# Layer 0 of a fused two-layer transformer kernel: projection moved ahead of two transposes on TensorE, exponentials moved up on ScalarE

## The chip, the cores and the metric

The kernel runs on one core of a Trainium2 chip. The metric is the device time of one execution in microseconds; the time of the kernel before is the median of three executions.

## The reference, cut to what matters

The input is x, 16 sequences of 512 rows of 128 numbers, float32. Two layers follow, each an attention block and a mixture-of-experts block with a residual sum and a layer norm behind each. The change touches only layer 0, whose attention runs between the 16 heads of one row (a 16x16 softmax per row, not between rows), so that rows are independent:

```python
qkv = einsum('bnm,fm->bnf', x, Wqkv)             # per row: 16 heads x (q, k, v) of 8
scores = einsum('bnhd,bngd->bnhg', q, k) / 8.0    # 16 x 16 for every row
attn = softmax(scores, axis=-1)
out = einsum('bnhg,bngd->bnhd', attn, v)
x1 = layernorm(x + out @ Wproj.T + bproj)
logits = x1 @ gate_w.T + gate_b                   # keep the top 2 of 8, softmax
x2 = layernorm(x1 + sum_e gate[e] * (x1 @ expert_w[e] + expert_b[e]))
```

Layer 1 (causal-masked attention with 16 heads, then a routed expert block) is not changed.

## The kernel before, in words

`layer0` (L66) works on pairs of 128-row tiles: 64 tiles, so NP = 32 pairs. It is software-pipelined over five stages: step s starts the attention scores of pair s, sums the heads and projects pair s-1, does the gates and expert products of pair s-2, sums the experts and does the second norm of pair s-3, and makes layer 1's value rows of pair s-4. Each engine has its own hand-written order of these pieces (a function `step` per engine); the flags `part[n]` say which stages exist in the first and last steps. Engines are tied by counting semaphores only, and each engine issues in its written order, so a piece that waits holds everything written behind it on the same engine. In the text, "the pair's" wait counts are left out.

The pieces that matter here, by engine:

- VectorE (DVE). `moments_1` (L639, L643) takes mean and variance of the projected rows in `ps_front` and waits for the projection's semaphore `r1_ps`. Then `exp_sums` (L735) and `exp_recips` (L742), which wait for ScalarE's exponentials; `qk_products` (L661, two of 2.2 us), `moments_2` (L651, L655), `gate` (L676 to L704), `qk_sums` (L713, 4.43 us), `find_max` (L719) and `shift_scores` (L726), which ends the step and sets `scores_shifted`.
- GpSimd (POOL). `inverse1` (L288 to L296) waits for `moments_1` and makes rstd and shift of the first norm; `normalise` (L266) makes the probabilities; `pv_products` (L274, two of 4.1 us) multiplies them with the values; `inverse2` (L302 to L310) and `bias_residual` (L316) follow.
- TensorE (PE). `sum_experts` (L422 to L429, of pair s-3) opens the step; it waits for `gT_sb` (the turned gates copied to SBUF) and for `scores_shifted`. Then `values` (L451), `turn_x1` (L388), `turn_r2` (L437), `logits` (L403, L405), `four_experts` (L396) for the first tile, `qkv_products` (L352), `sum_heads` of the first tile (L364, 16 transposes that accumulate), `qkv_products`, `four_experts(1, 0)`, `sum_heads` of the second tile, `four_experts(1, 1)`, and at the end of the step `turn_gates` (L414), `turn_x2` (L444) and `project` (L377, L379), which sets `r1_ps`. `turn_gates` and `project` both wait for `oT_sb`, the copy of the summed heads.
- ScalarE (ACT). The end of its step is `apply_gates(1, 0)` (L541), `norm2` (L562), `copy_oT` (L504, sets `oT_sb`), `copy_gT` (L549, sets `gT_sb`), `apply_gates(1, 1)` (L541), `copy_x2T` (L570) and `exponentials` (L511, two of 256 columns; each waits for its half of `scores_shifted`). The next step opens with `norm1` (L519), `copy_r2T` (L555) and `copy_x1T` (L526).
- SyncE loads `xT` and the residual rows two steps ahead and stores the turned second norm; its waits are on `qkv_ps`, `r1_ps` and `x2T_sb`.

The PSUM areas at stake: `ps_front` holds the projection (columns 0 to 255) and the logits, `ps_turn` the summed heads and, in its other half, in turn the turned x1 and the turned gates, `ps_scores` the scores and then the summed experts of another pair. So `sum_experts` can only write after the scores have been read by `shift_scores`.

Of the kernel before, what the change touches and what calls it, by code (L numbers as in the profile page):

```python
# [34 lines left out]
def when(eng, semaphore, count):  # L35

    if not isinstance(count, int) or count > 0:
        eng.wait_ge(semaphore, count)  # L38
# [27 lines left out]
def layer0(nc, sh, xT_in, wqkv, wproj, bproj, gate_w, gate_b, expert_w, expert_b, wv1, wqT, wkT, bq, keep):  # L66
# [7 lines left out]
    with ExitStack() as ctx:  # L74
# [116 lines left out]
        def before(u, j, k):  # L191

            return u + (j - k) // 2, (j - k) % 2

        def first(u, j, s):

            return isinstance(u, int) and 2 * u + j == s
# [3 lines left out]
        def tile(t, a, n=P):  # L201
            return t[:, a * n:(a + 1) * n]

        with nc.Block() as block:
# [129 lines left out]
            def _(pe):  # L334
                pe.wait_ge(wqkv_in, 16)

                def build_matrices():
                    pe.wait_ge(qk_weights_in, 16 * 3)
                    for g in range(H // 4):
                        for h in range(4 * g, 4 * g + 4):  # L340
                            mm = pe.matmul(tile(ps_m[g], h % 4), tile(wq, h), tile(wk, h), start=True, stop=True)
                        mm.then_inc(m_ps, 1)
                    pe.wait_ge(m_sb, 1)
                    for h in range(H):
                        mm = pe.matmul(ps_m[0][:, h:h + 1], tile(wk, h), bq_sb[:, h:h + 1], start=True, stop=True)
                    mm.then_inc(mb_ps, 1)
# [21 lines left out]
                def project(u, j):  # L368
                    s = 2 * u + j
                    pe.wait_ge(oT_sb, s + 1)  # L370
                    pe.wait_ge(xres_biased, s + 1)
                    if first(u, j, 0):
                        pe.wait_ge(m_sb, H // 4)
                    when(pe, x1_ready, 2 * s)
                    when(pe, gates_ready, s)
                    for a in range(2):
                        pe.matmul(tile(ps_r1, a), tile(attnT, a), wproj_sb[:, :], start=(a == 0), stop=False)  # L377
                    for a in range(2):
                        mm = pe.matmul(tile(ps_r1, a), tile(xres[j], a), ident[:, :], start=False, stop=(a == 1),  # L379
                                       is_transpose=True)  # L380
                    mm.then_inc(r1_ps, 1)
# [9 lines left out]
                def four_experts(u, j, a, half):  # L391
                    s = 2 * u + j
                    if first(u, j, 0):
                        pe.wait_ge(mb_sb, 1)
                    when(pe, gated_ready, 4 * s + 2 * a + half - 1)
                    pe.matmul(ps_y[half][:, :], tile(x1T, a), expw_sb[:, half * 4 * P:(half + 1) * 4 * P],  # L396
                              start=True, stop=True).then_inc(experts_ps, 1)
# [10 lines left out]
                def turn_gates(u, j):  # L408

                    s = 2 * u + j  # L410
                    pe.wait_ge(gates_ready, s + 1)
                    pe.wait_ge(oT_sb, min(s + 2, NP) if isinstance(s, int) else s + 2)
                    for a in range(2):
                        mm = pe.transpose(tile(ps_gT, a), tile(gates, a, E), ident[:, :])  # L414
                    mm.then_inc(gT_ps, 1)

                def sum_experts(u, j):

                    s = 2 * u + j
                    pe.wait_ge(gT_sb, s + 1)  # L420
                    pe.wait_ge(scores_shifted, 2 * min(s + 3, NP) if isinstance(s, int) else 2 * (s + 3))
                    pe.matmul(ps_r2T, expb_sb[:, :], gatesT[:, :], start=True, stop=False)  # L422
                    for a in range(2):
                        pe.matmul(tile(ps_r2T, a), tile(x1[j], a), ident[:, :], start=False, stop=False,
                                  is_transpose=True)
                        for e in range(E):
                            if e % 4 == 0:
                                pe.wait_ge(gated_ready, 4 * s + 2 * a + e // 4 + 1)
                            mm = pe.matmul(tile(ps_r2T, a), tile(gated[a], e), ident[:, :], start=False,  # L429
                                           stop=(a == 1 and e == E - 1), is_transpose=True)  # L430
                        mm.then_inc(r2T_ps, 1)
# [22 lines left out]
                def step(u, j, part):  # L454
                    if first(u, j, 1):
                        build_matrices()
                    if part[4]:
                        sum_experts(*before(u, j, 3))
                    if part[5]:
                        values(*before(u, j, 4))  # L460
                    if part[3]:
                        turn_x1(*before(u, j, 2))
                    if part[4]:
                        turn_r2(*before(u, j, 3))
                    if part[3]:
                        logits(*before(u, j, 2))
                        four_experts(*before(u, j, 2), 0, 0)
                        four_experts(*before(u, j, 2), 0, 1)
                    if part[0]:
                        qkv_products(*before(u, j, -1), 0)  # L470
                    if part[2]:
                        sum_heads(*before(u, j, 1), 0)
                    if part[0]:
                        qkv_products(*before(u, j, -1), 1)
                    if part[3]:
                        four_experts(*before(u, j, 2), 1, 0)
                    if part[2]:
                        sum_heads(*before(u, j, 1), 1)
                    if part[3]:
                        four_experts(*before(u, j, 2), 1, 1)  # L480
                        turn_gates(*before(u, j, 2))
                    if part[4]:
                        turn_x2(*before(u, j, 3))
                    if part[2]:
                        project(*before(u, j, 1))
                qkv_products(0, 0, 0)
                qkv_products(0, 0, 1)
                pe.wait_ge(consts_made, 5)
# [4 lines left out]
            def _(act):  # L493
# [6 lines left out]
                def copy_oT(u, j):  # L500
                    s = 2 * u + j
                    act.wait_ge(pv_summed, 2 * (s + 1))
                    when(act, r1_ps, s)
                    act.copy(attnT[:, :], ps_oT).then_inc(oT_sb, 1)  # L504

                def exponentials(u, j):
                    s = 2 * u + j
                    when(act, probs_ready, s)
                    for a in range(2):
                        act.wait_ge(scores_shifted, 2 * s + a + 1)  # L510
                        act.activation(tile(exps, a, HH), tile(shifted, a, HH), ACT.Exp, scale=0.125)\  # L511
                           .then_inc(exps_ready, 1)
# [76 lines left out]
                def step(u, j, part):  # L589
                    if first(u, j, 1):  # L590
                        copy_matrices()
                    if part[3]:
                        norm1(*before(u, j, 2))
                    if part[4]:
                        copy_r2T(*before(u, j, 3))
                    if part[3]:
                        copy_x1T(*before(u, j, 2))
                    if part[5]:
                        copy_v(*before(u, j, 4))
                    if part[3]:  # L600
                        gate_exp(*before(u, j, 2))
                    if part[0]:
                        copy_kv(*before(u, j, -1), 0)
                    if part[3]:
                        apply_gates(*before(u, j, 2), 0, 0)
                        apply_gates(*before(u, j, 2), 0, 1)
                    if part[0]:
                        copy_kv(*before(u, j, -1), 1)
                    if part[3]:
                        apply_gates(*before(u, j, 2), 1, 0)  # L610
                    if part[4]:
                        norm2(*before(u, j, 3))
                    if part[2]:
                        copy_oT(*before(u, j, 1))
                    if part[3]:
                        copy_gT(*before(u, j, 2))
                        apply_gates(*before(u, j, 2), 1, 1)
                    if part[4]:
                        copy_x2T(*before(u, j, 3))
                    if part[1]:  # L620
                        exponentials(u, j)
                copy_kv(0, 0, 0)
                copy_kv(0, 0, 1)
                steps(act, step)
# [1402 lines left out]
```

## Time and profile before

| what | value |
|---|---|
| median of 3 runs | 2204.5 us (2201.29 to 2204.99) |
| profiled execution | 2212.01 us, span 2210.3 us |
| busy in the span: PE, DVE, ACT, POOL | 93%, 81%, 71%, 48% |
| layer 0 in the span | about the first 550 us, 32 steps |

The profiled execution is one execution under the profiler, 1.7 us longer than its own span and 7.5 us above the median. In the rows below a time is counted from the start of the span, "us" is the busy time of a merged group, "x" the number of instructions in it, and the bracket at the end is the idle time of that engine just before the group and what ended it. PEld is TensorE's weight load, which can overlap its matmuls. Matmuls overlap one another by a part of their modelled length, so a group's cost is read from the start of one group to the start of the next.

### The profile page before, as it was taken

How to read it: one execution, taken by the hardware profiler on the slowest of the kernel's cores; microseconds unless marked ns; L12 is line 12 of the kernel's file. 1: busy time of each engine (PE TensorE's matmuls, PEld its weight loads, DVE VectorE, ACT ScalarE, POOL GpSimd, SP SyncE). 2: the span in 40 equal slices, each digit the busy share in tenths (PEclk: the TensorE clock that was granted, in tenths of full speed). 3: DMA queues.
4: the chain of work that ended last, by engine and by line, in shares of the span. 5: the costliest groups of instructions: out<-in, count | busy, mean ns of one | idle time of the engine just before them, and what ended most of it. 6: DMA issues, size and time to landing. Idle time of an engine off the chain costs nothing. (4 is left out here: it accounts for less than half of the span.)

```text
span 2210.3 us, 59748 instructions
## 1 busy us (share of the span) xinstructions
PE 2054.5 (93%) x16112; PEld 1527.0 (69%) x16112; DVE 1785.9 (81%) x5918; ACT 1559.9 (71%) x3951; POOL 1060.8 (48%) x2184
## 2 busy tenths in 40 slices
PE   7999999997999999999999999999999993999990
PEld 5666666665676766776676676676677663999990
DVE  7899999994788888888888888888888884677765
ACT  3565656565788877878787887787887872777764
POOL 5777777775223334344334334333434434444444
PEclk8999999999999999999999999999999996999995
DMA  2000000000000000000000000000200001222217
GB/s 76 23 23 27 21 28 21 28 21 15 13 2 9 4 11 11 2 12 11 3 10 11 7 6 11 9 4 11 88 2 11 11 3 39 66 65 63 67 57 228
DMA packets 63632, 62.84 MB, mean 28 GB/s; under 512 B 9834, under 2 KB 58613, under 8 KB 62855
## 3 DMA queue, kind: packets, MB, share of 16 engines
q1 hardware_dynamic: 54906, 42.64, 6.4%
q0 software_dynamic: 8448, 16.93, 2.2%
q8 instruction: 121, 1.98, 0.4%
q14 instruction: 157, 1.29, 0.2%
HBM read 33.17 MB, written 22.69 MB: 25 GB/s over the span
## 5 line engine op out<-in xcount | busy, mean ns | idle before, releaser
L1367 DVE SCALAR_TENSOR_TENSOR restT<-ps_t,leadT 128x512 f16<-128x512 f32 (+1 forms) x768 | 458.8, 597 | 135.1 <-ACT leadT L1294 97.7
L1294 ACT ACTIVATE leadT<-ps_t 128x512 f16<-128x512 f32 (+1 forms) x768 | 402.8, 525 | 131.8 <-PE ps_t L1168 131.7
L1151 PE MATMUL ps_s<-xT_all,qm 128*128 128x512 f32 (+1 forms) x1024 | 490.0, 560 | 0.8 <-ACT qm L1275 0.8
L1168 PEld LDWEIGHTS ps_t<-ident,p 128*128 128x128 f32 x2560 | 314.8, 141 | 238.7 <-issue 171.5
L1168 PE MATMUL ps_t<-ident,p 128*128 128x128 f32 x2560 | 415.2, 276 | 9.3 <-DVE restT L1367 5.8
L1285 ACT ACTIVATE p<-ps_s,neg_max 128x512 f32<-128x512 f32 (+1 forms) x512 | 326.1, 637 | 88.3 <-DVE neg_max L1357 74.2
L987 POOL CAST v_parts<-v_all 128x36 bf16<-128x36 f32 x256 | 57.4, 224 | 614.5 <-PE ps_o L1182 614.3
L1357 DVE CUSTOM_DVE_ANT_0 ps_s<-ps_s,mask 128x512 f32<-128x512 f32 (+1 forms) x512 | 319.8, 625 | 38.5 <-PE ps_s L1151 37.4
L1151 PEld LDWEIGHTS ps_low<-xT_all,qm 128*128 128x128 f32 x1024 | 194.6, 190 | 135.4 <-issue 122.2
L1142 PE MATMUL ps_qm<-xT_all,m_all 128*128 128x512 f32 x512 | 263.7, 597 | 3.2 <-PEq L765 3.2
L274 POOL TENSOR_TENSOR pv_prod<-probs,kv 128x2048 f32<-128x2048 f32 x64 | 259.5, 4076 | 3.8 <-POOL probs L266 2.3
L1668 POOL DMA_INDIRECT results<-row_out,row_in x136 | 133.7, 983 | 161.8 <-issue 121.0
L1151 PE MATMUL ps_low<-xT_all,qm 128*128 128x256 f32 (+1 forms) x1024 | 208.9, 326 | 0.0
L1275 ACT ACTIVATE qm<-ps_qm,mb_all 128x512 f32<-128x512 f32 x256 | 176.1, 688 | 43.2 <-PE ps_qm L1142 39.8
L1285 ACT ACTIVATE p<-ps_low,neg_max 128x256 f32<-128x256 f32 (+1 forms) x512 | 188.3, 428 | 0.1
L1357 DVE CUSTOM_DVE_ANT_0 ps_low<-ps_low,mask 128x256 f32<-128x256 f32 (+1 forms) x512 | 177.8, 387 | 9.7 <-PE ps_low L1151 1.4
L541 ACT ACTIVATE gated<-ps_y,gates 128x128 f32<-128x128 f32 x512 | 141.7, 371 | 44.1 <-DVE gates L704 41.6
L1789 DVE SCALAR_TENSOR_TENSOR e_hid<-e_ps_u,e_wide,e_silu 114x128 f32<-114x128 f32 x408 | 118.4, 345 | 60.3 <-ACT e_silu L1748 55.4
L1182 PE MATMUL ps_o<-v_parts,leadT 128*128 128x27 bf16 x2560 | 161.4, 175 | 0.9 <-DVE restT L1367 0.6
L1182 PE MATMUL ps_o<-v_parts,restT 128*128 128x27 bf16 x2560 | 160.6, 174 | 0.0
L1073 POOL DMA_INDIRECT rows_dram<-rows,slot_idx x128 | 128.9, 1007 | 63.8 <-issue 50.2
L1748 ACT ACTIVATE e_silu<-e_ps_g,e_wide 114x128 f32<-114x128 f32 x408 | 120.3, 366 | 54.4 <-PE e_ps_g L1701 51.0
(231 smaller groups left out, 4161.2 us busy)
## 6 DMA issues: line engine op xcount, KB each, us to landing
row_in<-rows_dram SPq DMA_DIRECT2D x136, 65.0 KB
y<-results SPq DMA_DIRECT2D x16, 512.0 KB, 5.3
xT<-in_xT SPq DMA_DIRECT2D x32, 128.0 KB, 2.1
xres<-in_xT SPq DMA_DIRECT2D x32, 128.0 KB, 2.1
xT_all<-x2T SPq DMA_DIRECT2D x32, 128.0 KB, 2.0
out_x<-x SPq DMA_DIRECT2D x16, 256.0 KB, 3.5
xT_all<-in_wide SPq DMA_DIRECT2D x1, 2760.0 KB
results<-row_out,row_in POOLq DMA_INDIRECT x136
```

What stands on the lines that cost most here:

```text
L274: pool.tensor_tensor(tile(pv_prod, a, HH * DH).rearrange("p (g h d) -> p g h d", g=H, d=DH), tile(probs, a, HH).rearrange("p (h g) -> p g ...
L541: last = act.activation(tile(gated[a], e), tile(ps_y[half], e % 4), ACT.Copy, scale=gates[:, a * E + e:a * E + e + 1])
L1142: pe.matmul(ps_qm[:, :], blk(m_all, h), xT_all[:, bass.ds(b * S, S)], start=True, stop=True).then_inc(qm_ps, 1)
L1151: mm = pe.matmul(ps_s[n], qm[j][:, n * P:(n + 1) * P], xT_all[:, bass.ds(b * S, (n + 1) * P)], start=True, stop=True)
L1168: mm = pe.transpose(ps_t[g][:, at + n * P:at + (n + 1) * P], probs[i][:, n * P:(n + 1) * P], ident[:, :])
L1182: mm = pe.matmul(out_ps[:, i, :], part[:, at + n * P:at + (n + 1) * P], v_parts[j][:, n * PARTS * PV:(n + 1) * PARTS * PV], start=(n == 0 ...
L1275: act.activation(qm[j][:, :], ps_qm[:, :], ACT.Identity, bias=mb_all[:, h:h + 1], scale=SCALE).then_inc(qm_sb, 1)
L1285: act.activation(probs[i][:, :], ps_s[i], ACT.Exp, bias=neg_max[:, i:i + 1], scale=-1.0).then_inc(probs_ready[i], 1)
L1294: act.activation(leadT[j][g][:, :], ps_t[g][:, 0:width[g]], ACT.Copy, scale=RAISE)\
L1357: dve.tensor_tensor_reduce(out=ps_s[i], in0=ps_s[i], in1=mask[:, S - n:S], scale=-1.0, scalar=3e38, op0=ALU.add, op1=ALU.min, accum_out=ne ...
L1367: dve.scalar_tensor_tensor(out=restT[j][g][:, :], in0=ps_t[g][:, 0:width[g]], scalar=RAISE, in1=leadT[j][g][:, :], op0=ALU.mult, op1=ALU.s ...
L1668: pool.indirect_dma_start(out=results[:, :], out_offset=bass.IndirectOffsetOnAxis(ap=row_in[r][:, P + 1:ROW].bitcast(U32), axis=0), in_=ro ...
```

## The change

On TensorE `project` of pair s-1 moves from the end of the step to just behind `four_experts(1, 1)`, ahead of `turn_gates` and `turn_x2`. On ScalarE `exponentials` of pair s moves from the end of the step to just behind `copy_oT`, ahead of `copy_gT`, `apply_gates(1, 1)` and `copy_x2T`. No instruction is added or removed, and every wait stays with its instruction.

```diff
@@ -478,11 +478,12 @@
                         sum_heads(*before(u, j, 1), 1)
                     if part[3]:
                         four_experts(*before(u, j, 2), 1, 1)
+                    if part[2]:
+                        project(*before(u, j, 1))
+                    if part[3]:
                         turn_gates(*before(u, j, 2))
                     if part[4]:
                         turn_x2(*before(u, j, 3))
-                    if part[2]:
-                        project(*before(u, j, 1))
                 qkv_products(0, 0, 0)
@@ -612,13 +613,13 @@
                         norm2(*before(u, j, 3))
                     if part[2]:
                         copy_oT(*before(u, j, 1))
+                    if part[1]:
+                        exponentials(u, j)
                     if part[3]:
                         copy_gT(*before(u, j, 2))
                         apply_gates(*before(u, j, 2), 1, 1)
                     if part[4]:
                         copy_x2T(*before(u, j, 3))
-                    if part[1]:
-                        exponentials(u, j)
                 copy_kv(0, 0, 0)
```

## Rows read from the trace of the kernel before

**Rows 1.** Busy time in one window, 26 steps of layer 0; PEclk is the granted clock.

```profile
core 0: us, PE busy (x) PEld busy (x) DVE busy (x) ACT busy (x) POOL busy (x), PEclk, DMA share, GB/s
99.64:511.98 412.34, 382.63 (x2285) 268.53 (x2284) 376.60 (x780) 242.66 (x857) 315.32 (x312) 1.00 0.08 25
```

**Rows 2.** Waits, 99 to 497 us: who waited for whom, total us, times, longest.

```profile
POOL var L288 <- DVE mv L643: 86.5, 25, 3.6
...
DVE stats L639 <- PE ps_front L379: 11.9, 26, 0.5
...
DVE exp_sum L735 <- ACT exps L511: 2.4, 13, 0.2
```

**Rows 3.** Waits of VectorE, 40 to 99 us, in the first steps.

```profile
DVE stats L639 <- PE ps_front L379: 5.2, 3, 3.0
```

**Rows 4.** Timeline of VectorE: start us, busy us, group, [idle before, releaser].

```profile
98.88 0.76 DVE L726 TENSOR_TENSOR shifted<-ps_scores,score_max 128x256 f32<-128x256 f32 x2
...
306.34 0.50 DVE L639 BATCH_NORM_STATS2 stats<-ps_front 128x6 f32<-128x128 f32 x2 [0.43 <-PE ps_front L379]
...
321.00 0.76 DVE L726 TENSOR_TENSOR shifted<-ps_scores,score_max 128x256 f32<-128x256 f32 x2
322.26 0.49 DVE L639 BATCH_NORM_STATS2 stats<-ps_front 128x6 f32<-128x128 f32 x2 [0.51 <-PE ps_front L379]
...
511.23 0.75 DVE L726 TENSOR_TENSOR shifted<-ps_scores,score_max 128x256 f32<-128x256 f32 x2
```

**Rows 5.** Timeline of GpSimd, one step and the start of the next.

```profile
307.45 0.20 POOL L288 TENSOR_TENSOR var<-mv,eps_pair 128x2 f32<-128x2 f32 x1 [3.59 <-DVE mv L643]
...
309.96 8.12 POOL L274 TENSOR_TENSOR pv_prod<-probs,kv 128x2048 f32<-128x2048 f32 x2 [0.18 <-POOL probs L266]
...
323.27 0.20 POOL L288 TENSOR_TENSOR var<-mv,eps_pair 128x2 f32<-128x2 f32 x1 [3.33 <-DVE mv L643]
...
325.66 8.11 POOL L274 TENSOR_TENSOR pv_prod<-probs,kv 128x2048 f32<-128x2048 f32 x2
```

**Rows 6.** Timeline of TensorE's matmuls, the same step and the next.

```profile
318.14 1.97 PE L364 MATMUL ps_turn<-ident,pv_prod 128*128 128x128 f32 x16
319.94 1.02 PE L396 MATMUL ps_y<-expw_sb,x1T 128*128 128x512 f32 x2
320.80 0.38 PE L414 MATMUL ps_turn<-ident,gates 128*8 128x128 f32 x2
...
321.24 0.61 PE L377 MATMUL ps_front<-wproj_sb,attnT 128*128 128x128 f32 x4
...
322.00 0.69 PE L422 MATMUL ps_scores<-gatesT,expb_sb 8*128 8x256 f32 x2
...
324.64 0.61 PE L451 MATMUL ps_turn<-wv_sb,x2T 128*128 128x128 f32 x4
325.55 0.44 PE L388 MATMUL ps_turn<-ident,x 128*128 128x128 f32 x2 [0.29 <-ACT x L519]
...
327.31 1.96 PE L396 MATMUL ps_y<-expw_sb,x1T 128*128 128x512 f32 x4
329.11 0.81 PE L352 MATMUL ps_qkv<-wqkv_sb,xT 128*128 128x384 f32 x2
```

**Rows 7.** Timeline of TensorE's weight loads in the step after, one row.

```profile
336.34 0.08 PEld L414 LDWEIGHTS ps_turn<-ident,gates 128*8 128x8 f32 x1 [0.43 <-ACT attnT L504]
```

**Rows 8.** Weight loads of line 377, 99 to 497 us: ns min/median/max.

```profile
L377 PEld LDWEIGHTS ps_front<-wproj_sb,attnT x104: 186/192/192, 98.9 to 496.0; 128*128 128x128 f32 x104
```

**Rows 9.** Timeline of ScalarE around the end of the same step.

```profile
321.22 0.36 ACT L549 COPY gatesT<-ps_turn 8x256 f32<-8x256 f32 x1 [0.65 <-PE ps_turn L414]
321.49 1.10 ACT L541 ACTIVATE gated<-ps_y,gates 128x128 f32<-128x128 f32 x4
...
322.76 0.72 ACT L511 ACTIVATE exps<-shifted 128x256 f32<-128x256 f32 x2
324.69 0.81 ACT L519 ACTIVATE x<-ps_front,shift,rstd 128x128 f32<-128x128 f32 x2 [1.21 <-POOL shift L296]
```

## The prediction

> **What bounds the kernel now.** I read four views, in this order. First the busy windows: over 26 steps of layer 0 TensorE is busy 383 of 412 us and VectorE 377, at a granted clock of 1.00, the 2.4 GHz level [rows 1]. Neither share says which of them sets the step. Second, the waits: VectorE waits for the projection in each of 26 steps, 11.9 us in all, and 13 times for the exponentials, 2.4 us; GpSimd waits 86.5 us for VectorE's moments [rows 2]. Third, the timelines of the engines over one step, to find a closed loop: a chain of waits that comes back to the same instruction one step later. Fourth, the ends of steps: from the 98.88 to the 511.23 row of L726 lie 26 steps, 15.86 us each [rows 4].
>
> The loop closes through GpSimd, TensorE and VectorE. GpSimd's `inverse1` starts at 307.45, its head products end at 309.96 + 8.12 = 318.08: 10.63 us [rows 5]. TensorE's `sum_heads` follows at 318.14 (0.06), `four_experts(1,1)` at 319.94 (1.80), `turn_gates` at 320.80 (0.86), `project` at 321.24, past `turn_gates` and `turn_x2` (0.44) [rows 6]. VectorE's statistics start at 322.26 (1.02) [rows 4], and GpSimd's next `inverse1` at 323.27 (1.01) [rows 5]. The sum is 15.82, the distance of the two `inverse1` rows, with no slack in any link. The steps alternate a little, so I use the mean of 15.86. VectorE has slack: after `shift_scores` ends, which I call E (321.00 + 0.76 = 321.76, and 306.34 - 0.43 = 305.91 a step earlier), it is idle 0.51 and 0.43 us [rows 4].
>
> **The change, part by part.**
>
> 1. *`project` ahead of `turn_gates` and `turn_x2`.* In the loop the link of 0.44 us goes: 15.86 becomes 15.42. Its waits move with it. `oT_sb` was waited for by `turn_gates` as well, so nothing new stands ahead of it; in the step after the one shown that copy ended last before the first weight load [rows 7]. The projection's first weight load now stands directly behind that copy: 0.19 us [rows 8] in place of 0.08 [rows 7]. If all is exposed, 0.11 us in every second step, 0.05 per step; if hidden, 0. I take 0.05, since the load did start only after the copy: **15.47 us per step**. The Trainium skill ("TensorE: Matmul & The Clock Gate", the table at its head) says that TensorE pulls weight loads ahead of matmuls in flight; by that rule the load would cost nothing and the step would be 15.42. In the row of the trace the load didn't pass its own wait, so I hold to the row.
>
> 2. *`turn_gates`, `turn_x2` behind it.* They start some 0.8 us later in the stream (the projection's own length, 322.00 - 321.24 [rows 6]), but nobody but ScalarE waits for them: `copy_gT` and `copy_x2T`. The next point covers both.
>
> 3. *`exponentials` ahead of `copy_gT`, `apply_gates(1,1)` and `copy_x2T`.* Gain: the sum of exponentials on VectorE no longer waits, 2.4 us in 13 waits [rows 2], but VectorE is not the loop that binds, so in the sum this is 0; it lowers VectorE's own bound. Cost: ScalarE now stands from the end of `copy_oT` until the shifted scores come at E, and `copy_gT` behind it. The second exponential starts about E + 0.1 (as `norm1` at 324.69 stood 0.1 behind its releaser), both take 0.72, so the second 0.36, then `copy_gT` 0.36, and 0.08 until TensorE [rows 9]: `sum_experts` starts at **S = E + 0.9**, where it was E + 0.24 (322.00) [rows 6]. It waited for the shifted scores before too, so 0.66 us is lost there, and TensorE stands behind it. `apply_gates(1,1)` takes 1.10 [rows 9] and then ends about S + 1.1; `sum_experts` needs it only for its last four of 18 transposes, over 2 us after S, so it doesn't bind. SyncE's store of x2 comes later with `copy_x2T` and the residual load earlier with `r1_ps`; the first has a whole step before its buffer is used again, the second is waited for a step later. Both cost 0; should that cover fail, a load takes 2 us and would be seen as a wait of POOL L316 or ACT L570.
>
> 4. *Who is behind S.* TensorE from S on: `sum_experts` 2.64 (322.00 to 324.64), `values` until 325.25, then `turn_x1`, which waited 0.29 for `norm1` and started at 325.55; 1.76 to `four_experts` at 327.31; 1.80 to `qkv_products` at 329.11, 0.81 at most; `sum_heads` 1.80; `qkv_products` 0.81; `four_experts(1,0)` 0.86; and then the second `sum_heads` [rows 6]. Without waits that is 3.25 + 1.76 + 1.80 + 0.81 + 1.80 + 0.81 + 0.86 = 11.08 us, so `sum_heads` can start at S + 11.1 = E + 12.0. Today it starts at E + 12.23 (318.14 - 305.91). The closed loop that this makes takes two steps: 12.0 to `sum_heads`, 1.80 and 0.86, 1.02 to the statistics, and from there VectorE's own work to the next E, 321.76 - 306.34 = 15.42 (0.16 of it is the wait for exponentials in every second step, so 15.34): 31.02 / 2 = 15.51. Taken with 0.65 for each `qkv_products` (three quarters of the 0.86 of a 512-column product, 384 columns [rows 6]), it is 15.35. So this loop is as long as the first within a tenth, and `norm1` is no part of it, since it waits for GpSimd's shift [rows 9].
>
> 5. *VectorE alone.* Its own work is 15.34 plus 0.03 between instructions: 15.37 us. No step can be shorter.
>
> **Sum.** The step is the longest of 15.47, 15.35 to 15.51, and 15.37: I take 15.47, from 15.86, 0.39 us over 26 steps, 10.1 us. The first steps wait for the projection too, three times [rows 3]; each gives 0.44: 1.3 us. In the last two steps VectorE has nothing to hide behind; there the earlier projection may give up to 0.44 and the later `sum_experts` take as much, I take 0. Together 11.4 us. Against the profiled execution's own 2212.0 that is 2200.6; the median of the runs shown is 7.5 lower, 2204.5, so **2193 us**. Everything behind layer 0 only starts earlier.
>
> **Rivals.**
>
> - *Partly given back.* `sum_experts` starts later than E + 0.9, say E + 1.2 by slower hand-overs between ScalarE and TensorE, and the two-step loop gives 15.65: 0.21 times 26 and 1.3, some 7 us, 2197.5. For it: the tie within a tenth. Against it: my sum for that loop already takes busy lengths. Chance 0.15.
> - *No change.* The moved wait takes the gain: S at E + 1.5 gives 15.8 us per step, 2202. It shows as `turn_x1` waiting for nothing, and VectorE's wait for the projection as long as now. Chance 0.11. The part of the change on TensorE would then have been worth 0.44, and the part on ScalarE cost it.
> - *VectorE as the bound.* If the longer weight load is hidden and GpSimd's products follow at once, the step is 15.37: 0.49 times 26 and 1.3, 14 us, 2190.5. I count it with the forecast.
> - *Slower.* The place is ScalarE between `copy_oT` and `copy_gT`. Written order makes `copy_gT` stand behind a wait for VectorE's last instruction of the step; the two-step loop passes today's 31.76 as soon as S is over E + 1.65. Should `sum_experts` in effect also need `apply_gates(1,1)` and `copy_x2T` (1.10 and 0.35 later, E + 2.35), the loop is 32.5, the step 16.2, 0.36 longer, and with 26 steps 9 us are added: 2214. Against it: the row of `copy_gT` is 0.36 long and nothing else stands ahead of it. Chance 0.06. The Trainium skill ("TensorE: Matmul & The Clock Gate", the table at its head) says that ScalarE's queue is strictly first in, first out; that is what makes this rival possible, and the rows of the kernel before can't show it, as `copy_gT` there stands behind nothing that waits.
>
> **How the numbers follow.** The forecast, a step of 15.37 to 15.55 us, has 0.68. With 0.15 for the part given back, faster by more than 0.2% (4.4 us, about what a measurement of this kernel tells from no change) has 0.83, within 0.2% has 0.11, slower 0.06. The predicted time is the likeliest case's. The range goes from VectorE's bound of 15.37 with the last steps' gain and the runs' own spread of 2 us, 2188, to just short of no change, 2202; about 2 in 10 is left out above and a little below.
>
> **What would show it.** Right: in the new profile VectorE's wait at L639 falls from 0.46 us a step to about 0.1, its wait at L735 is gone, L377 starts directly behind L396, and steps are 15.4 to 15.5 us apart. ScalarE waits at L511 for L726 instead of at L549, TensorE waits about 0.5 us at L422 for ScalarE's `gatesT`, and less than before at L388 for x1. Right too if GpSimd's wait at L288 gets shorter by about the step's gain. The forecast is wrong if TensorE's second `sum_heads` starts later than 0.1 to 0.2 us behind GpSimd's products in most steps: then the loop over `sum_experts` has taken over. It is wrong in another way if the steps get shorter and the total doesn't, or if the granted clock leaves 1.00 in layer 0, now that TensorE has a new gap ahead of `sum_experts`.

## The result, and the profile after

The changed kernel takes 2186.64 us (median of 4 runs, 2185.8 to 2188.25) where the kernel before took 2204.74 (median of 4 in the same session): a ratio of 0.9923, 95% interval 0.9911 to 0.9934. Faster, as forecast, but by 18.1 us where 11.4 had been worked out, and 1.4 us below the range.

The profiled execution took 2186.65 us (span 2184.9), so it stands for its median. That of the kernel before, 2212.0, stood 7.3 us above its own, and the two spans must not be compared whole.

Busy times of the changed kernel in the window of [rows 1]; the last column but two is the granted clock:

```profile
99.64:511.98 412.34, 385.71 (x2354) 278.39 (x2354) 375.26 (x800) 254.52 (x880) 323.98 (x322) 1.00 0.08 24
```

The shares hardly move; more instructions fit into the same window (2354 matmuls for 2285), which now reaches 18.8 us past the last `shift_scores`. Waits of the changed kernel, 99 to 497 us, answering to [rows 2]:

```profile
POOL var L288 <- DVE mv L644: 77.2, 26, 3.1
...
ACT exps L512 <- DVE shifted L727: 23.3, 26, 0.9
...
PEld ps_turn L364 <- POOL pv_prod L274: 21.2, 27, 1.0
...
PE ps_scores L422 <- ACT gatesT L550: 13.1, 26, 0.5
...
DVE stats L640 <- issue: 2.1, 12, 0.2
...
DVE stats L640 <- PE ps_front L379: 0.3, 1, 0.3
```

VectorE's wait for the projection falls from 11.9 us to 0.3 us under its name and 2.1 us that the profile calls "issue", 0.1 us a step together (the probe below shows that these too are the projection); its wait for the exponentials is gone, ScalarE now waits for VectorE at the exponentials (0.9 us a step), and TensorE waits 0.5 us a step for `gatesT` at the start of `sum_experts`. All four were forecast.

VectorE's timeline of the changed kernel, answering to [rows 4]:

```profile
93.70 0.75 DVE L727 TENSOR_TENSOR shifted<-ps_scores,score_max 128x256 f32<-128x256 f32 x2
...
309.02 0.76 DVE L727 TENSOR_TENSOR shifted<-ps_scores,score_max 128x256 f32<-128x256 f32 x2
309.84 0.50 DVE L640 BATCH_NORM_STATS2 stats<-ps_front 128x6 f32<-128x128 f32 x2
...
324.23 0.75 DVE L727 TENSOR_TENSOR shifted<-ps_scores,score_max 128x256 f32<-128x256 f32 x2
325.15 0.49 DVE L640 BATCH_NORM_STATS2 stats<-ps_front 128x6 f32<-128x128 f32 x2 [0.17 <-issue]
...
493.21 0.75 DVE L727 TENSOR_TENSOR shifted<-ps_scores,score_max 128x256 f32<-128x256 f32 x2
```

From 93.70 to 493.21 lie the same 26 steps as in [rows 4]: 399.5 us where it was 412.35, so 12.8 us came from there, 0.49 per step (15.37 for 15.86). The sixth step itself ends 5.2 us earlier (93.70 for 98.88). Together the last `shift_scores` is 18.0 us earlier. So all of the 18 us is in layer 0, and 5.2 us of it in its first steps, where I had put 1.3.

The loop in the changed kernel, first on GpSimd, then TensorE's matmuls, then the weight loads of `project`:

```profile
310.85 0.20 POOL L288 TENSOR_TENSOR var<-mv,eps_pair 128x2 f32<-128x2 f32 x1 [2.89 <-DVE mv L644]
...
313.24 8.11 POOL L274 TENSOR_TENSOR pv_prod<-probs,kv 128x2048 f32<-128x2048 f32 x2
```

```profile
320.33 1.13 PE L396 MATMUL ps_y<-expw_sb,x1T 128*128 128x512 f32 x2
321.40 1.97 PE L364 MATMUL ps_turn<-ident,pv_prod 128*128 128x128 f32 x16
323.21 1.02 PE L396 MATMUL ps_y<-expw_sb,x1T 128*128 128x512 f32 x2
324.07 0.61 PE L377 MATMUL ps_front<-wproj_sb,attnT 128*128 128x128 f32 x4
324.51 0.38 PE L379 MATMUL ps_front<-ident,xres 128*128 128x128 f32 x2
324.73 0.38 PE L414 MATMUL ps_turn<-ident,gates 128*8 128x128 f32 x2
324.95 0.38 PE L444 MATMUL ps_tail<-ident,x 128*128 128x128 f32 x2
325.86 0.47 PE L422 MATMUL ps_scores<-gatesT,expb_sb 8*128 8x256 f32 x1 [0.53 <-ACT gatesT L550]
```

```profile
323.88 0.60 PEld L377 LDWEIGHTS ps_front<-wproj_sb,attnT 128*128 128x128 f32 x4 [0.48 <-ACT attnT L505]
```

`inverse1` at 310.85, the products end at 321.35 (10.50), `sum_heads` 0.05 behind, `four_experts` 1.81, `project` 0.86, the statistics (325.15) 1.08. The projection follows the expert product directly, and no link has slack: this is still the loop that sets the step. `sum_experts` starts at E + 0.88 (325.86 against 324.98), where the forecast had E + 0.9.

### The profile page after: what moved, and what is told of

Same layout as the page of the kernel before. It is cut to its first block and busy times, and to the rows that moved or that the text cites. A ratio compares the mean times of both kernels' runs of the same rounds, so it can differ in the third digit from the quotient of the medians.

```text
span 2184.9 us, 59761 instructions
## 1 busy us (share of the span) xinstructions
PE 2037.5 (93%) x16112; PEld 1524.8 (70%) x16112; DVE 1778.6 (81%) x5918; ACT 1563.4 (72%) x3951; POOL 1060.6 (49%) x2184
## 5 line engine op out<-in xcount | busy, mean ns | idle before, releaser
L1358 DVE CUSTOM_DVE_ANT_0 ps_low<-ps_low,mask 128x256 f32<-128x256 f32 (+1 forms) x512 | 177.2, 386 | 12.6 <-PE ps_low L1152 1.8
```

What stands on the lines that cost most here:

```text
L1358: dve.tensor_tensor_reduce(out=ps_s[i], in0=ps_s[i], in1=mask[:, S - n:S], scale=-1.0, scalar=3e38, op0=ALU.add, op1=ALU.min, accum_out=ne ...
```

## The experiments

Two questions: do the parts add up and which loop binds now, and where do the first steps' 5.2 us come from? The kernels before and after were also run again as they are, under other names; the ratios are against the kernel before on the same chip.

**TensorE's move alone.**

```diff
                         four_experts(*before(u, j, 2), 1, 1)
+                    if part[2]:
+                        project(*before(u, j, 1))
+                    if part[3]:
                         turn_gates(*before(u, j, 2))
                     if part[4]:
                         turn_x2(*before(u, j, 3))
-                    if part[2]:
-                        project(*before(u, j, 1))
```

> Theory A (the two moves need each other): the gates are turned 0.8 us later, so copy_gT, apply_gates(1,1), copy_x2T and behind them the exponentials end some 6.3 us behind GpSimd's head products; with 0.9 us to the reciprocals and 9.35 us to the next products a new loop of 16.6 us per step takes over from 15.86: about 20 us slower than before, 2225, and VectorE waits over 1 us per step at the sum of exponentials. Rival B (the moves are independent, TensorE's is worth 0.44 per step alone): 2192.

Measured 2220.68 us, ratio 1.0076 (1.0062 to 1.0090): slower by 17 us, where about 20 was expected. ScalarE's timeline of this kernel and then its waits, 99 to 490 us:

```profile
308.89 0.37 ACT L505 COPY attnT<-ps_turn 128x256 f32<-128x256 f32 x1
310.64 0.36 ACT L550 COPY gatesT<-ps_turn 8x256 f32<-8x256 f32 x1 [1.37 <-PE ps_turn L414]
...
311.92 0.35 ACT L571 COPY x2T<-ps_tail 128x256 f32<-128x256 f32 x1
312.17 0.72 ACT L512 ACTIVATE exps<-shifted 128x256 f32<-128x256 f32 x2
```

```profile
ACT gatesT L550 <- PE ps_turn L414: 31.5, 23, 1.4
DVE exp_sum L736 <- ACT exps L512: 28.9, 24, 1.3
POOL probs L266 <- DVE exp_rec L743: 22.8, 24, 1.0
```

The gates are turned later, ScalarE stands 1.37 us for them with the exponentials behind it, VectorE waits for these and GpSimd for VectorE. The steps are 16.47 us apart, where 16.6 was expected. The early projection by itself is a loss.

**ScalarE's move alone.**

```diff
                         copy_oT(*before(u, j, 1))
+                    if part[1]:
+                        exponentials(u, j)
                     if part[3]:
                         copy_gT(*before(u, j, 2))
                         apply_gates(*before(u, j, 2), 1, 1)
                     if part[4]:
                         copy_x2T(*before(u, j, 3))
-                    if part[1]:
-                        exponentials(u, j)
```

> Theory A: the loop over GpSimd, TensorE and the statistics is untouched, 15.86 us per step, so no change within 2 us of before (2203 to 2207), though VectorE's wait at the sum of exponentials is gone and its wait at the statistics grows by as much. Rival B (the later sum of experts costs time by itself): slower by 0.1 to 0.3 us per step, 2208 to 2213.

Measured 2200.2 us, ratio 0.9989 (0.9980 to 0.9998), 3.5 us below the kernel before and about 3 us below the range expected. The steps give little of it: they are 15.82 us apart, 0.04 less, about 1 us in all. The rest fits a better start of 6 of the 11 runs (2199.42 to 2200.2; see the first steps below), though no trace shows the start of those six. VectorE's wait at the statistics took over what it had waited for the exponentials, as expected (99 to 490 us of this kernel; the kernel before has 11.6 there):

```profile
DVE stats L639 <- PE ps_front L379: 13.4, 25, 0.6
```

In the steps by itself a trifle, together with the other move it turns a loss of 0.6 us per step into a gain of 0.49. The two parts aren't two terms of a sum; the second is what makes the first pay.

**One pair of transposes back in the loop.**

```diff
                         four_experts(*before(u, j, 2), 1, 1)
+                        turn_gates(*before(u, j, 2))
                     if part[2]:
                         project(*before(u, j, 1))
-                    if part[3]:
-                        turn_gates(*before(u, j, 2))
```

> Both moves, but turn_gates stays ahead of project: 0.22 us more on TensorE in the loop over GpSimd and the statistics. Theory (that loop and VectorE's own work are both at 15.38 in the changed kernel, tied): the step is 15.38 plus 0.15 to 0.22, so 4 to 6 us over the changed kernel, 2190.5 to 2192.5, and VectorE waits at the statistics again, 0.15 to 0.25 per step. Rival (VectorE alone sets the step, the loop has slack of 0.2 or more): 2186.

Measured 2197.7 us, ratio 0.9972 (0.9963 to 0.9982). The steps are 15.64 us apart, 0.26 more than in the changed kernel for 0.22 us of work, and VectorE waits 0.37 us a step for the projection. Per step that is a bit over the theory's upper end, and the rival's slack of 0.2 us is not there: the loop has no slack at all. The median is 5 us above the 2190.5 to 2192.5 expected. Against a trace of the changed kernel that began alike (`after_third`, below) layer 1 starts 7.6 us later, 545.46 for 537.84; the rest of the 11 us between the medians fits how often the runs had the better start.

**A third of a microsecond more on VectorE.** One more reciprocal behind `exp_recips`, its result not used.

```diff
                     dve.reciprocal(exp_rec[:, :], exp_sum[:, :]).then_inc(recips_ready, 1)
+                    dve.reciprocal(probe[:, :], exp_sum[:, :])
```

> The changed kernel with one more reciprocal of 128x32 on VectorE behind exp_recips (its result is not used), 0.27 to 0.35 us per step, outside the loop over GpSimd. Theory (VectorE's own work sets the step as much as that loop): 0.27 to 0.35 times 30 more, 8 to 10.5 us, 2194.5 to 2197. Rival (only the loop over GpSimd and TensorE sets it): within 1.5 us of 2186.3.

Measured 2187.69 us, 1.4 over the changed kernel's 2186.3: the rival's answer, and my theory of a tie fell. VectorE's timeline of this kernel, and then TensorE's matmuls:

```profile
311.55 0.75 DVE L728 TENSOR_TENSOR shifted<-ps_scores,score_max 128x256 f32<-128x256 f32 x2
312.23 0.50 DVE L641 BATCH_NORM_STATS2 stats<-ps_front 128x6 f32<-128x128 f32 x2
...
314.04 0.30 DVE L745 RECIPROCAL probe<-exp_sum 128x32 f32<-128x32 f32 x1
314.25 4.42 DVE L663 TENSOR_TENSOR qk_prod<-ps_qkv,kv 128x2048 f32<-128x2048 f32 x2
```

```profile
322.93 1.13 PE L397 MATMUL ps_y<-expw_sb,x1T 128*128 128x512 f32 x2
323.89 1.91 PE L365 MATMUL ps_turn<-ident,pv_prod 128*128 128x128 f32 x16
325.64 1.02 PE L397 MATMUL ps_y<-expw_sb,x1T 128*128 128x512 f32 x2
326.50 0.61 PE L378 MATMUL ps_front<-wproj_sb,attnT 128*128 128x128 f32 x4
```

The probe takes 0.21 us of issue (314.04 to 314.25), and the steps are 15.44 us apart, 0.06 more. Here the statistics start 0.07 us *before* the shifted scores end (312.23 against 311.55 + 0.75), or level with that end in every second step; in the changed kernel they start 0.06 or 0.17 behind it. Those gaps, which the profile calls no wait or "issue", were the wait for the projection: in the changed kernel the statistics start 1.02 or 1.08 us behind `project`, the same as in the kernel before, where the profile names it. VectorE's own work is thus at most 15.44 - 0.21 = 15.23 us a step, not 15.37, and the changed kernel stands at least 0.15 us above it.

This doesn't show that VectorE alone sets the step of the probed kernel, because there too the statistics start 1.02 or 1.08 us behind `project`. What sets it is a third loop, which neither the prediction nor the theory above had: from the statistics over the probe to the end of VectorE's `gate` 9.31 us, to ScalarE's `apply_gates(0, 0)` 0.19, to TensorE's `four_experts(1, 0)` 1.20, `sum_heads` 0.96, `four_experts(1, 1)` 1.75, `project` 0.86, and to the statistics (327.58) 1.08. That is 15.35 us for this step and by the same links 15.54 for the next, 15.44 in the mean. The second `sum_heads` starts 0.15 us behind GpSimd's products (323.89 against 323.74) instead of 0.05. In the changed kernel `sum_heads` stood 1.07 behind `four_experts(1, 0)` (320.33 to 321.40), so there this loop had slack: it takes 15.23 where the step is 15.38, and of the probe's 0.21 us only 0.06 came through.

**`copy_gT` ahead of the exponentials**, both moves kept.

```diff
                         copy_oT(*before(u, j, 1))
+                    if part[3]:
+                        copy_gT(*before(u, j, 2))
                     if part[1]:
                         exponentials(u, j)
                     if part[3]:
-                        copy_gT(*before(u, j, 2))
                         apply_gates(*before(u, j, 2), 1, 1)
```

> Both moves, but copy_gT stays ahead of the exponentials on ScalarE: the sum of experts starts some 0.3 us earlier and the exponentials end about 0.7 us later. Theory (TensorE's later sum of experts has slack, and VectorE needs the exponentials only 0.9 us behind its last shifted scores): same as the changed kernel within 1.5 us, 2185 to 2188. Rival (the later sum of experts is what sets the step): 0.1 to 0.3 us per step faster, 2178 to 2183. Second rival (the exponentials have no slack): slower, 2190 or more.

The steps are 15.38 us apart, as in the changed kernel, though `sum_experts` starts 0.25 us earlier (E + 0.6). So the loop over `sum_experts` doesn't bind. The median is 2190.5, outside the 2185 to 2188 expected; its best run is 2185.23. The difference lies in the first steps: its trace is level with the trace of the changed kernel that began alike (`after_third`), layer 1 starting at 537.39 against 537.84.

**The first steps.** The two kernels again, unchanged:

> The kernel before, unchanged, for a second trace. If the earlier start of the third step in the trace of the changed kernel (3.2 us at the end of step 2) came from TensorE's clock in the first 60 us and not from the change, this trace has another split: granted clock in 20 to 60 us differs by trace, and the start of the first projection (33.31 us in the first trace, 30.11 in the changed kernel's) moves with it. If it came from the change, it is 33.3 again. Steps behind 100 us are 15.86 us apart either way.

> The changed kernel, unchanged, for a second trace: steps 15.38 us apart behind 100 us; the first projection starts at 30.1 us if the first steps gained by the change, at 30 to 33.5 if by the clock. Ratio to before 0.992 as in the first runs.

> The changed kernel once more, for how often its runs start with TensorE at the higher level. If the start is chance and alike in both kernels, most of these runs lie near 2188 to 2190, as most runs of the kernel before lie near 2204 (7 of 53 at 2200.5 or below). If the changed kernel starts well more often for a reason of its own, most lie at 2185.5 to 2186.7, as 7 of its 9 did.

Windows of the kernel before in its first trace, in its second, and of the changed kernel in `after_again` and `after_third`; the third number from the end is the granted clock, 1.00 the level of 2.4 GHz:

```profile
20.00:30.00 10.00, 10.00 (x59) 9.29 (x58) 7.80 (x5) 1.73 (x4) 7.48 (x3) 0.66 0.01 2
...
50.00:60.00 10.00, 9.00 (x45) 5.88 (x45) 8.14 (x24) 3.91 (x13) 7.25 (x7) 0.87 0.05 16
```

```profile
20.00:30.00 10.00, 9.54 (x79) 8.67 (x78) 7.79 (x5) 2.66 (x7) 7.48 (x3) 1.00 0.01 2
30.00:40.00 10.00, 6.17 (x18) 3.71 (x19) 8.60 (x23) 2.10 (x7) 7.89 (x7) 0.66 0.08 26
...
50.00:60.00 10.00, 9.02 (x39) 5.43 (x38) 9.55 (x20) 4.68 (x16) 9.92 (x7) 0.83 0.01 2
```

```profile
20.00:30.00 10.00, 9.54 (x78) 8.67 (x77) 7.86 (x5) 2.85 (x8) 7.55 (x3) 1.00 0.01 2
30.00:40.00 10.00, 6.17 (x19) 3.62 (x18) 8.79 (x23) 1.91 (x6) 8.08 (x7) 0.66 0.09 26
...
50.00:60.00 10.00, 9.57 (x51) 5.84 (x50) 9.55 (x20) 5.32 (x20) 9.84 (x7) 1.00 0.01 2
```

```profile
20.00:30.00 10.00, 10.00 (x59) 9.29 (x59) 7.84 (x5) 1.73 (x4) 7.52 (x3) 0.67 0.01 2
```

Each kernel has two starts. In one the clock falls to the lower level within 20 to 30 us, while TensorE runs the one-column products of L345; in the other it falls only in the next ten, where TensorE waits for the first norms. Nothing that the change moves has run by then. A trace between the two exists: in `vector_probe` the clock fell at about 25 us, behind those products. With the start alike:

| trace | clock, 20 to 30 us | sixth `shift_scores` | last | first product of layer 1 |
|---|---|---|---|---|
| before, first | 0.66 | 98.88 | 511.23 | 551.99 |
| after_third | 0.67 | 97.69 | 497.11 | 537.84 |
| before_again | 1.00 | 95.17 | 507.27 | 547.99 |
| after_again | 1.00 | 93.13 | 492.59 | 533.34 |

The change is worth 14.15 us with the one start and 14.65 with the other: 12.6 to 12.9 in the 26 steps, 1.2 to 2.0 ahead of them. The starts of a pair are alike to 0.3 us only (the first projection begins at 33.31 and 33.59, and at 29.87 and 29.68; in `after_third` the clock was at the lower level before 20 us too); with that taken off, the change is worth 14.4 and 14.5. The start itself is worth 4.0 and 4.5 us. The gain ahead of the 26 steps lies mostly in the fifth step, 1.3 us shorter in both pairs. The clock may have a part in what came ahead of the 26 steps: between 52 and 62 us it falls to the lower level for some 3 us in all three traces of the kernel before (the third is `before_filled`, below) and in none of the changed kernel, 0.83 against 1.00 between 50 and 60 us in the windows above. No run separates this from the shorter wait.

The medians were 2203.46 and 2186.27 for the second runs and 2186.94 for the third, 16.5 to 17.2 us apart. The kernel before has 8 of the 62 runs beside these experiments at 2200.5 us or below and most near 2204; the changed kernel has 10 of 14 at 2185.5 to 2187 and 4 at 2188 to 2191. Read as starts, by analogy with the traced runs, this says that the changed kernel had the better one more often, and that is the other 2 to 4 us. Compared within a cluster, the distance is the 14 us of the table: the fastest run of the kernel before is 2199.62, that of the changed kernel 2185.55. Whether the change brings the better start about, the runs don't tell: going by their times the kernel before had it in 3 of the 11 runs of `before_again`, `exps_only` in 6 of 11, `copy_gT` ahead of the exponentials in 1 of 6 and `project` behind the gates in 1 of 9.

**The start made alike.** Sixteen products between the one-column ones, in both kernels, their results not used.

```diff
                     for h in range(H):
+                        pe.matmul(tile(ps_m[0], 1), tile(wk, h), tile(wk, h), start=True, stop=True)
                         mm = pe.matmul(ps_m[0][:, h:h + 1], tile(wk, h), bq_sb[:, h:h + 1], start=True, stop=True)
```

> The kernel before with 16 more products of 128 columns between the one-column products of L345 in step 1 (their results are not used), some 3.5 us more of TensorE there. If the clusters of the kernel before (2199.6 to 2200.4 and 2203.5 to 2206) come from the clock falling behind those one-column products, the granted clock stays at 1.00 from 20 to 30 us, the runs form one cluster, and the median is 2200 plus 0 to 3.5. If not, the two clusters remain, and everything is up to 3.5 later.

> The changed kernel with the same filling. If the change is worth 14.7 us where the clock of the first 60 us is alike (12.6 in the steps behind 100 us and 2.0 ahead of them), this is 14.7 below the filled kernel before, within 1; if the change is worth the 17.4 of the medians by itself, it is 17.4 below.

Measured 2204.48 us (11 runs, 2203.5 to 2205.98) and 2190.33 (5 runs, 2189.91 to 2191.33): one narrow cluster each, 14.15 us apart, where 14.7 was expected within 1. (The traces of the two are 15.0 apart at the first product of layer 1, 552.45 and 537.41, of which 12.8 us lie in the 26 steps.) So the change's own worth is 14 to 15 us. The kernel before came out 1 us above the 2203.5 that was to be its limit. The granted clock is 0.99 and 1.00 from 20 to 30 us, as expected, but falls behind it in both (0.86 and 0.83 from 30 to 40 us).

**Work in the wait of the first norm.** Both moves, and three unused products of 512 columns ahead of the first pair's `turn_x1`.

```diff
                 def turn_x1(u, j):
                     s = 2 * u + j
+                    if first(u, j, 0):
+                        for _ in range(3):
+                            pe.matmul(ps_y[1][:, :], ident[:, :], expw_sb[:, 0:4 * P], start=True, stop=True)
```

> The changed kernel with three products of 512 columns (not used, 0.86 us each) in TensorE's 3.4 us wait ahead of the first turn_x1. If the fall of the granted clock from 30 to 40 us, behind that wait, costs what the longer expert products show (3.52 in place of 1.96 us), the clock stays at 1.00 from 34 us on in a trace that started well, and the best runs are 1 to 2.5 us below 2185.6. Rival: TensorE isn't what the third step waits for, so nothing is gained, 2185.5 to 2188; or the products themselves delay turn_x1, 2187 to 2189.

Measured 2185.01 us (5 runs, 2184.72 to 2187.72), ratio to before 0.9919 (0.9905 to 0.9932), the lowest median of all; against the changed kernel's 0.9926 in the same session that is within the intervals, so a gain of the whole kernel isn't shown. The trace, one of the worse start, shows the mechanism. TensorE's matmuls of this kernel, and then of `after_third`, which has the same start:

```profile
34.09 2.74 PE L387 MATMUL ps_y<-expw_sb,ident 128*128 128x512 f32 x6
37.63 0.44 PE L391 MATMUL ps_turn<-ident,x 128*128 128x128 f32 x2 [0.79 <-ACT x L523]
...
39.32 1.96 PE L399 MATMUL ps_y<-expw_sb,x1T 128*128 128x512 f32 x4
```

```profile
37.89 0.69 PE L388 MATMUL ps_turn<-ident,x 128*128 128x128 f32 x2 [3.37 <-ACT x L520]
...
40.45 3.76 PE L396 MATMUL ps_y<-expw_sb,x1T 128*128 128x512 f32 x4
```

With the wait filled the expert products take 1.96 us instead of 3.76, and layer 1 begins at 535.37 instead of 537.84, 2.5 us earlier, of which 0.3 us was there at the first projection (33.33 for 33.59). The best run is 0.8 us below the changed kernel's best (2184.72 against 2185.55), just short of the 1 to 2.5 us expected; no trace shows the clock of a better start with the wait filled.

## Why the prediction was right or wrong

*What bounds the kernel*: right, before and after. The loop over GpSimd, `sum_heads`, `project` and the statistics set the step, and still does: 0.22 us put back in it costs 0.26, and 0.21 put on VectorE outside it costs 0.06.

*Part 1, the 0.44 us*: right. What failed is the size of the term for the steps, the forecast of **15.47 us per step**; it is 15.37 to 15.38. Half of the error is the 0.05 that I added for the exposed weight load. The load starts behind `attnT` (323.88), but beside the expert product that is still streaming, and the projection follows that product by the 0.86 us that this takes (323.21 to 324.07 above). By the rule of the Trainium skill ("TensorE: Matmul & The Clock Gate", the table at its head), that weight loads are pulled ahead of matmuls in flight, the load was to cost nothing, and here the trace agrees. The step of [rows 7] showed it already: that load at 336.34 came behind its copy too, and `turn_gates` still started 0.86 us behind the product (335.72 and 336.58 below). The other half is that the gain was some 0.05 over 0.44. In every second step before, TensorE reached `sum_heads` late, as these matmuls of the kernel before show:

```profile
333.01 1.12 PE L396 MATMUL ps_y<-expw_sb,x1T 128*128 128x512 f32 x2 [0.53 <-ACT gated L541]
333.97 1.91 PE L364 MATMUL ps_turn<-ident,pv_prod 128*128 128x128 f32 x16
335.72 1.02 PE L396 MATMUL ps_y<-expw_sb,x1T 128*128 128x512 f32 x2
336.58 0.38 PE L414 MATMUL ps_turn<-ident,gates 128*8 128x128 f32 x2
```

The products had ended at 333.77, but `four_experts(1,0)` had come only at 333.01, released by ScalarE's gated products, and `sum_heads` could follow only 0.96 later: 0.20 us behind the products, where the changed kernel has 0.05 in both kinds of step. That is the third loop, through `gate`, which bound every second step before. I had looked at the loop over GpSimd in one kind of step and taken the mean of both. Over 26 steps the term is 12.6 to 12.9 us, not 10.1.

*Parts 3 and 4*: right. `sum_experts` at E + 0.88 against E + 0.9, and its loop isn't binding, as the experiment with `copy_gT` shows. The rivals "partly given back", "no change" and "slower" placed at this spot didn't come. What the prediction lacked is that ScalarE's move had to come along: I gave it "in the sum 0", and alone it is, but without it TensorE's move costs 17 us.

*Part 5, VectorE alone at 15.37*: wrong by at least 0.14. I took all of the distance from statistics to E as work and only added to it; the probe gives 15.23 at most. It did no harm to the sum, but the tie that I stated between the loops was never there, and the 15.37 that was measured is the loop over GpSimd: that it equals the figure for VectorE as the bound is a coincidence.

*The first steps*: 1.3 us forecast, 1.2 and 2.0 with like starts, 2.2 in the filled pair. Small, though the 0.44 in each of three waits isn't how it came: the fifth step alone gave 1.3.

*The sum*: 11.4 forecast, 14.15 to 14.65 with like starts and 14.15 in the filled pair. From the median before that alone would be 2190, inside the range. The rest, 3.5 to 4 us up to 18.1, is what the prediction had no term for at all: **TensorE's clock in the first 30 us**. I read "PEclk 1.00" for the steady steps and took the first steps' rows as they were, although the kernel before shows 0.86 from 20 to 80 us. A term of 4 us with two values, spread unevenly over the two kernels' runs, stood beside a range that went 2 us below its lowest case. The traces show that the start is worth this much; that the medians differ by it is read from the clusters of the runs, and why the changed kernel began better more often stays open.

## What to carry to other kernels

In a pipeline over several engines, search the closed loop of waits and time each link in every kind of step; a link that is removed gives what it measures, and an idle gap of 0.05 to 0.2 us that the profile doesn't name can still be the wait that sets the step. When a probe costs less than its own length, look for the loop that took over, in the other traces too. Ask of each moved piece what its followers hold back on the next engine: the early projection paid only because the exponentials no longer stood behind the gates. And before a difference of a few microseconds is explained, take a second trace of each kernel and compare executions that began alike.

## What the runs showed of the hardware that had not been expected

- The granted clock fell to the 1.2 GHz level while TensorE was busy 10.00 of 10 us, with the 32 one-column matmuls of L345 (4.83 us for all of them, against 3.63 where it stayed up). With wide matmuls put between them it stayed at 0.99 to 1.00 over the same ten microseconds. The one-column products don't always bring the fall: in `before_again` and `after_again` they ran at 1.00.
- The same kernel starts in two ways, with 4.0 to 4.5 us between them by the first product of layer 1. The runs of one kernel fall in clusters, as 2185.5 to 2187 and 2188 to 2191 here. Why one kernel has the better start more often than another is open.
- Layer 1 up to its first expert product, untouched, took 1315.5 us in the first trace of the kernel before (551.99 to 1867.49), 1310.6 in the second and 1311.2 to 1311.6 in the three traces of the changed kernel, on top of the start. Its cause is open. So a single trace's span can be off by a third of what this change is worth.
